# Stores of gathered rows in blocks of 128 nodes, loads in parts of 112 and 13 partitions

## The reference

```python
edge_index = jnp.stack([src, dst])
x = x + gnn0(_layernorm(x), W, bias, src, dst, edge_weight)      # segment_sum(h[dst] * w, src)
x = x + moe0(_layernorm(x), 8 experts 256->256->256, top 2)
x = x + gnn1(_layernorm(x), edge_index, edge_weight, ...)         # 3 layers
x = x + moe1(_layernorm(x), shared 256->1024->256 and 8 experts, top 2)

# gnn1
h = x @ W_in + b_in
for l in range(3):
    msgs = edge_weight[:, None] * h[col]
    pooled = segment_sum(msgs, row) + h
    hid = relu(bn(pooled @ W1[l] + b1[l]))
    h = relu(bn(hid @ W2[l] + b2[l]))
```

## Time and profile before

| | us |
|---|---|
| median of 3 runs | 2988.94 |
| profiled execution | 2990.68 |
| its span | 2988.8 |
| TensorE matmul busy | 2341.4 (78%) |
| VectorE busy | 1330.6 (45%) |
| ScalarE busy | 946.7 (32%) |
| POOL busy | 1418.9 (47%) |
| mean granted clock of TensorE | 0.889 |

### The profile page before, as it was taken

One profiled execution on the slowest core, in us unless ns is written; L12 is line 12 of the kernel. 1 busy time (PEld: TensorE's weight loads), 2 busy tenths in 40 slices (PEclk: granted clock), 3 DMA queues, 4 the chain that ended last, 5 costly groups with the idle time before them and its releaser, 6 DMA issues. The chain is left out here.

```text
span 2988.8 us, 52339 instructions
## 1 busy us (share of the span) xinstructions
PE 2341.4 (78%) x14004; PEld 2098.9 (70%) x14004; DVE 1330.6 (45%) x3733; ACT 946.7 (32%) x2732; POOL 1418.9 (47%) x1465
## 2 busy tenths in 40 slices
PE   1989959999868766776567766567775899999999
PEld 0789959888767635675446766356664689999988
DVE  6789976666443353444334443434443441111122
ACT  4368858788012241000120000300000433333332
POOL 1377767776004355777417777147775001111142
PEclk9999979999859978888789897788986799999999
DMA  2100023333029833333313333133333249999932
GB/s 77 40 4 3 3 65 102 105 105 98 15 82 301 288 105 91 104 104 105 67 64 105 104 105 105 20 110 105 104 105 72 64 163 327 326 328 326 310 91 61
DMA packets 243386, 363.22 MB, mean 122 GB/s; under 512 B 57437, under 2 KB 188486, under 8 KB 242886
## 3 DMA queue, kind: packets, MB, share of 16 engines
q1 hardware_dynamic: 173780, 194.88, 20.1%
q0 software_dynamic: 66240, 163.71, 19.8%
q10 hardware_dynamic: 3250, 3.20, 0.3%
HBM read 322.49 MB, written 38.69 MB: 121 GB/s over the span
## 5 line engine op out<-in xcount | busy, mean ns | idle before, releaser
L749 POOL DMA_INDIRECT z_or_messages<-h_rows,agg_idx x768 | 729.6, 950 | 358.4 <-issue 224.9
L780 PE MATMUL ps<-z_or_messages 128*128 128x125 f32 x3072 | 484.7, 322 | 284.0 <-DMA z_or_messages<-h_rows,agg_idx 238.8
L780 PEld LDWEIGHTS ps<-z_or_messages 128*128 128x128 f32 x3072 | 450.7, 232 | 324.3 <-issue 250.7
L807 DVE TENSOR_TENSOR h_features<-h_features,ps 128x250 f32 x384 | 159.2, 414 | 514.8 <-PE ps L780 477.0
L722 ACT CAST agg_idx<-slots 128x4 int32 x264 | 51.7, 196 | 1042.5 <-PE ps L780 541.2
L1380 POOL DMA_INDIRECT moe_room<-h_rows,moe_inverse x112 | 106.0, 946 | 558.1 <-PE ps L1470 394.0
L749 POOL DMA_INDIRECT agg_room<-h_rows,agg_idx x256 | 248.9, 972 | 96.7 <-issue 70.8
L574 POOL DMA_INDIRECT payloads<-pay_st,idx_st x192 | 215.4, 1122 | 164.5 <-DMA idx_st<-slot_i 112.4
L1638 ACT ACTIVATE moe_room<-ps,moe_b 128x128 f32<-128x128 f32 x560 | 163.2, 367 | 366.4 <-PE ps L1482 366.4
L1482 PE MATMUL ps<-moe_room 128*128 128x128 f32 x2240 | 272.9, 277 | 7.0 <-issue 4.5
L1482 PEld LDWEIGHTS ps<-moe_room 128*128 128x128 f32 x2240 | 260.5, 193 | 13.5 <-issue 8.0
(11 more groups left out here) (285 smaller groups left out, 3263.2 us busy)
## 6 DMA issues: line engine op xcount, KB each, us to landing
moe_room<-in_L_ffn_W1p_dram SPq DMA_DIRECT2D x56, 1024.0 KB, 6.7
moe_room<-in_L_ffn_W2p_dram SPq DMA_DIRECT2D x56, 1024.0 KB, 7.6
moe_room<-in_L_ffn_w_dram SPq DMA_DIRECT2D x112, 256.0 KB, 5.0
expert_out<-moe_room SPq DMA_DIRECT2D x112, 128.0 KB, 6.0
z_or_messages<-h_rows,agg_idx POOLq DMA_INDIRECT x768, 2.7
h_rows<-moe_xn SPq DMA_DIRECT2D x10, 625.0 KB
h_rows<-layer_rows SPq DMA_DIRECT2D x10, 625.0 KB
agg_room<-h_rows,agg_idx POOLq DMA_INDIRECT x256
```

Source lines behind the costliest of these rows:

```text
L749: self.pg.nc.gpsimd.indirect_dma_start(self.G[:, k, :], None, self.pg.H, bass.IndirectOffsetOnAxis(ap=self.idx[:, k:k + 1], axis=0)).then_ ...
L780: last = nc.tensor.matmul(out[:, c, :], self.G[:, k, c * 128:(c + 1) * 128], self.S[:, k, :], start=(u == 0), stop=(u == PAIR - 1))
L807: nc.vector.tensor_tensor(a, a, p, ALU.add).then_inc(self.s_acc, 1)
```

## The change

Two things are changed.

1. The loads of src, dst, edge_weight and x go through `spread`: one transfer for partitions 0 to 111 (EVEN = 125 // 16 * 16 = 112) and one for 112 to 124. The waits are for twice the count.
2. The rows that are gathered in the network (three times: at the end of the first mixture and in layers 0 and 1) are made in 25 blocks of 128 consecutive nodes, the last of 53, and stored with one transfer each. In the mixture a block is made with the chunk that completes it, and the copies go into `got_second` on all 128 partitions. In the layers the buffers become a ring of ROWS = 10 single blocks, [128, 10, 256], each with a semaphore of its own; the copies wait for the store ten blocks back. A block that reaches into a chunk waits for that chunk's relu.

The first graph layer's rows (L322) and the rows that the two mixtures store for themselves (L1311) stay as they were.

```diff
+ROWS = 10
+ROW_BLOCKS = [(s, min(128, N - s)) for s in range(0, N, 128)]
+EVEN = P // 16 * 16
...
+def spread(eng, dst, src, sem):
+    for part in (slice(0, EVEN), slice(EVEN, P)):
+        eng.dma_start(dst[part], src[part]).then_inc(sem, 16)
...
-                sp.dma_start(src_i[:], src.rearrange("(p j) -> p j", p=P)).then_inc(ld_edge, 16)
-                sp.dma_start(dst_i[:], dst.rearrange("(p j) -> p j", p=P)).then_inc(ld_edge, 16)
-                sp.dma_start(slot_f[:], edge_weight.rearrange("(p j) -> p j", p=P)).then_inc(ld_edge, 16)
-                sp.dma_start(pg.X[:], x.rearrange("(j p) d -> p j d", p=P)).then_inc(ld_x, 16)
+                spread(sp, src_i[:], src.rearrange("(p j) -> p j", p=P), ld_edge)
+                spread(sp, dst_i[:], dst.rearrange("(p j) -> p j", p=P), ld_edge)
+                spread(sp, slot_f[:], edge_weight.rearrange("(p j) -> p j", p=P), ld_edge)
+                spread(sp, pg.X[:], x.rearrange("(j p) d -> p j d", p=P), ld_x)
...
-                dve.wait_ge(ld_edge, 48)
+                dve.wait_ge(ld_edge, 96)
...
-                act.wait_ge(ld_x, 16)
+                act.wait_ge(ld_x, 32)
...
+            ends = [0] + [sum(s0 + n <= c0 + m for s0, n in ROW_BLOCKS) for c0, m in CHUNKS]
+            self.row_blocks = [range(a, b) for a, b in zip(ends, ends[1:])]
...
-            for j in range(NT):
+            for j, (s0, n) in enumerate(ROW_BLOCKS):
                 sp.wait_ge(self.s_ro, j + 1)
-                sp.dma_start(pg.H[j * P:(j + 1) * P, :], self.rows[:, j, :]).then_inc(self.s_rst, 16)
-            sp.wait_ge(self.s_rst, 16 * NT)
+                sp.dma_start(pg.H[s0:s0 + n, :], self.got_second[0:n, j, :]).then_inc(self.s_rst, 16)
+            sp.wait_ge(self.s_rst, 16 * len(ROW_BLOCKS))
...
-                    last = nc.tensor.matmul(ps[0:P, 6 + j % 2, 0:D], net.h[:, k, j * P:(j + 1) * P], net.W[:, 1, k, :],
+                    last = nc.tensor.matmul(ps[0:n, 6 + j % 2, 0:D], net.h[:, k, s0:s0 + n], net.W[:, 1, k, :],
...
-                a.copy(self.rows[:, j, :], ps[0:P, 6 + j % 2, 0:D]).then_inc(self.s_ro, 1)
+                a.copy(self.got_second[0:n, j, :], ps[0:n, 6 + j % 2, 0:D]).then_inc(self.s_ro, 1)
...
-        self.rows = sb("rows2", [P, 2, U, D])
+        self.rows = sb("rows2", [128, ROWS, D])
...
-        for j in range(NT):
-            if j * P % CH == 0:
-                pe.wait_ge(ready, KD * (j * P // CH + 1))
+        for j, (s0, n) in enumerate(ROW_BLOCKS):
+            pe.wait_ge(ready, KD * -(-(s0 + n) // CH))
...
-            if j % U == 0 and q >= 2:
-                dve.wait_ge(self.s_st[q % 2], 16 * (q // 2))
+            if j >= ROWS:
+                dve.wait_ge(self.s_st[j % ROWS], 16 * (j // ROWS))
...
-        for q in range(NT // U):
-            sp.wait_ge(self.s_row, U * (q + 1))
-            sp.dma_start(self.pg.H[q * U * P:(q + 1) * U * P, :].rearrange("(j p) d -> p j d", p=P),
-                         self.rows[:, q % 2, :, :]).then_inc(self.s_st[q % 2], 16)
-        for h in range(2):
-            sp.wait_ge(self.s_st[h], 16 * ((NT // U + 1 - h) // 2))
+        for j, (s0, n) in enumerate(ROW_BLOCKS):
+            sp.wait_ge(self.s_row, j + 1)
+            sp.dma_start(self.pg.H[s0:s0 + n, :], self.rows[0:n, j % ROWS, :]).then_inc(self.s_st[j % ROWS], 16)
+        for u in range(ROWS):
+            sp.wait_ge(self.s_st[u], 16 * ((len(ROW_BLOCKS) - u + ROWS - 1) // ROWS))
```

More of the change, by code:

```diff
@@ L1559, in product, with rows @@
                 last.then_inc(self.s_p, 1)
-        def rows(c, j0, n):
+        def rows(c):
             pe.wait_ge(self.s_h, (c + 1) * KD)
-            for j in range(j0, j0 + n):
+            for j in self.row_blocks[c]:
+                s0, n = ROW_BLOCKS[j]
                 if j >= 2:
@@ L1576, in net_tensor @@
             if c:
-                rows(*self.groups[c - 1])
-        rows(*self.groups[G - 1])
+                rows(c - 1)
+        rows(G - 1)
     def net_psum(self, c, fo, n):
@@ L1648, in net_scalar, with rows @@
         a, ps, net = self.pg.nc.scalar, self.pg.ps, self.net
-        def rows(c, j0, n):
-            for j in range(j0, j0 + n):
+        def rows(c):
+            for j in self.row_blocks[c]:
+                n = ROW_BLOCKS[j][1]
                 act.wait_ge(self.s_r, j + 1)
-                a.copy(self.rows[:, j, :], ps[0:P, 6 + j % 2, 0:D]).then_inc(self.s_ro, 1)
+                a.copy(self.got_second[0:n, j, :], ps[0:n, 6 + j % 2, 0:D]).then_inc(self.s_ro, 1)
         act.wait_ge(net.s_w, net.loads)
@@ L1675, in net_scalar @@
             if c:
-                rows(*self.groups[c - 1])
-        rows(*self.groups[-1])
+                rows(c - 1)
+        rows(len(self.groups) - 1)
     def vector(self, dve):
@@ L1867, in __init__ @@
         self.s_out, self.s_tr, self.s_row, self.s_zero = (sem(n) for n in ("relu_out", "trd", "row", "zeroed"))
-        self.s_st = [sem(f"st{s}") for s in range(2)]
+        self.s_st = [sem(f"st{s}") for s in range(ROWS)]
         self.G = KD * len(CHUNKS)
@@ L1956, in rows_product @@
             for k in range(KD):
-                last = self.pg.nc.tensor.matmul(self.pg.ps[0:P, j % BANKS, 0:D], src[:, k, j * P:(j + 1) * P],
+                last = self.pg.nc.tensor.matmul(self.pg.ps[0:n, j % BANKS, 0:D], src[:, k, s0:s0 + n],
                                                 weight[:, k, :], start=(k == 0), stop=(k == KD - 1))
@@ L1967, in rows_out @@
     def rows_out(self, dve):
-        for j in range(NT):
+        for j, (s0, n) in enumerate(ROW_BLOCKS):
             dve.wait_ge(self.s_tr, j + 1)
-            q = j // U
-            if j % U == 0 and q >= 2:
-                dve.wait_ge(self.s_st[q % 2], 16 * (q // 2))
-            self.pg.nc.vector.tensor_copy(self.rows[:, q % 2, j % U, :], self.pg.ps[0:P, j % BANKS, 0:D]
+            if j >= ROWS:
+                dve.wait_ge(self.s_st[j % ROWS], 16 * (j // ROWS))
+            self.pg.nc.vector.tensor_copy(self.rows[0:n, j % ROWS, :], self.pg.ps[0:n, j % BANKS, 0:D]
                                           ).then_inc(self.s_row, 1)
     def rows_store(self, sp):
-        for q in range(NT // U):
-            sp.wait_ge(self.s_row, U * (q + 1))
-            sp.dma_start(self.pg.H[q * U * P:(q + 1) * U * P, :].rearrange("(j p) d -> p j d", p=P),
-                         self.rows[:, q % 2, :, :]).then_inc(self.s_st[q % 2], 16)
-        for h in range(2):
-            sp.wait_ge(self.s_st[h], 16 * ((NT // U + 1 - h) // 2))
+        for j, (s0, n) in enumerate(ROW_BLOCKS):
+            sp.wait_ge(self.s_row, j + 1)
+            sp.dma_start(self.pg.H[s0:s0 + n, :], self.rows[0:n, j % ROWS, :]).then_inc(self.s_st[j % ROWS], 16)
+        for u in range(ROWS):
+            sp.wait_ge(self.s_st[u], 16 * ((len(ROW_BLOCKS) - u + ROWS - 1) // ROWS))
     def rows_add(self, dve, X):
```

## The result

The changed kernel takes 2958.53 us, the median of 4 runs (2956.87 to 2963.87), against 2988.63 before in the same company (2987.89 to 2990.93, 4 runs); ratio 0.9896, 95% interval 0.9884 to 0.9908. The forecast was 2958.6. The profiled execution took 2959.41 us with a span of 2957.6, 31.2 less than before.

A forecast was written before the change was run, and what follows sets the result against it. It took each stage's own last chain before its barrier as the bound, in the first stage x's transfer. Terms -19.7 + 0.4 - 5.5 - 5.5 = -30.3 us, from the median 2988.94, gave 2958.6, range 2949 to 2968.

The forecast's parts named there:

- The bound and the engines: First stage bound by x's transfer; a transfer uses the largest number of engines up to 16 that divides its partitions.
- Rival A: First stage: splitting x brings nothing and only the layers gain, -10.6 us, so 2978 us; chance 6%.
- the direct price: First stage: VectorE's 2.4 us wait for the edges goes, so its first scan ends at 43.0 instead of 45.44.
- x: First stage: x split over 16 engines lands at 19.3 us instead of 39, and VectorE goes on 19.7 us sooner.
- 12.1 us at the expert loop's 315 GB/s: First stage: time for the 3.8 MB of x and edges on 16 engines, at the rate seen in the expert loop.
- 4.7 for the zeroing: First stage: POOL's zeroing of a table takes 4.7 us of every engine while x loads.
- the bound of 15.0: First stage: the gain if the table's zeroing slows x by twice the 4.7 us.
- The mixture's end: End of the first mixture: last store of 53 rows on one engine takes 2.3 us, tail 2.9 + 2.3 against 4.8, +0.4.
- The layers: Layers 0 and 1: no row store queues and copies keep TensorE's pace, -5.5 us in each.
- the 2.9 of fixed time: Tail from last copy to next load: what remains of 4.8 us without the stores' 1.1 and 0.8.
- the 0.4 for the semaphores: Layers' tail: 0.4 us for eight more semaphores that SP waits on.
- The clock rivals B and C: Second mixture: B, clock rises sooner, 2945 us, chance 5%; C, it rises later, 2999 with 80 us, chance 3%.

The follow-up runs named there:

- the run with 64 + 61: The changed kernel with x loaded in 64 + 61 partitions instead of 112 + 13; 3015.82 us (one run).
- the split tail: The changed kernel with the last block's 53 rows stored as 48 + 5 rows in two transfers; 2953.53 us, ratio 0.9876.

## Why the prediction was right, and where its terms were not

**The bound and the engines: right.** That 125 partitions use five engines and 112 use sixteen was read from shares of 0.34 and 0.94; the run with 64 + 61 and the packet counts show it. Rival A is out: loads alone gave 14.6 us. The rule of the Trainium skill on transfers to disjoint partition halves (DMA: Bandwidth & Descriptors, "Rules for kernel authors"), that they are not worth the trouble, fails here, because its premise that each already uses all the engines does not hold for 125 partitions.

**Edges: the direct price was right** in the changed kernel's trace (scan's end 42.92 against 43.0; in the other runs with split edges up to 43.95), but their larger part was missed. Split edges also let x be complete 4.7 us sooner, by the reading above because unsplit ones load five of the engines more than the rest.

**x: mis-sized by 4.1 us, the largest error.** The failed step is "12.1 us at the expert loop's 315 GB/s", plus 4.7 for the zeroing. Without the zeroing 3.8 MB take 21.69 - 2.5 = 19.2 us, and the zeroing costs 1.7 us. The two errors had opposite signs, +7.1 and -3.0. Of the 7.1 some 3.7 are the rate (240 GB/s would make it 15.8 us) and the remaining 3.4 the slow end behind 17 us, which the forecast did not have at all. The gain was 15.6 us, near the bound of 15.0, but that bound had been drawn for a dearer zeroing, which did not come.

**The mixture's end:** +0.4 was forecast, -0.3 measured at the tail. What the row block costs that moves to the last group can't be read: the stretch around it varies by 6 us.

**The layers: right in kind, 0.6 us short each.** From the first copy to the next load 6.1 and 6.0 us were won, forecast 5.5. The tail after the last copy was put at 5.6 and is 4.65; 2.3 for the 53 rows is what the split tail gave back, so the over-estimate lies in the 2.9 of fixed time and the 0.4 for the semaphores. No row stood behind that 0.4; the layers' tails are 0.14 us longer than the mixture's, where one semaphore is waited on (0.2 with 48 + 5). The third and fourth stretch gained 0.9 to 1.0 us more, ahead of the copies; that is not explained, and among kernels that are alike there this part varies by 1.1 and 0.6 us. Likewise the 0.9 us at the end of the span.

**The sum** was met within 1 us because x came 4.1 us (at the stage's end 4.5) short and all else gained 5.4 us more than forecast, 1.5 of it in the stretch that varies. The method was right, the exactness was luck. The clock rivals B and C did not come. In the second mixture (columns as in rows 2):

```profile
2360.00:2370.00 10.00, 10.00 (x36) 8.65 (x36) 7.59 (x19) 5.89 (x10) 0.00 (x0) 0.66 0.34 121
```

A mean of 0.66 puts the rise to 1.00 at 2366.8 us, against 2397.2 before by the same working: 30.4 us sooner, and the load that opens the last aggregation came 30.3 us sooner. The last stretch kept its length to 0.9 us.

## What to carry to other kernels

Look at the DMA share while one transfer runs: here 0.34 at full demand meant that the shape of the transfer, not the memory, was the limit, and a split at 112 partitions, a multiple of 16, mended it. Mind the remainder too: 53 leftover rows on one engine cost 2.3 us at each barrier more than 48 + 5. Do not take the full rate from another part of the kernel as the rate of the mended transfer, allow for an end at which some engines are done before others, and let the consumer wait in pieces where it works in pieces.

## What the runs showed of the hardware that was not expected

Sixteen engines reading x in rows of 1 KB move 230 to 262 GB/s, twice and not three times what five of them do, while their busy share is 1.1; with rows that lie together, 25 KB to a partition, it is 230 GB/s from 7 to 11 us at a share of 0.89 to 0.93. In the same kernel other loads run at 315 over 400 us, and with the zeroing beside x the same engines move 386 GB/s in all from 13 to 15 us. None of three things explains it by itself, neither the place of the rows, nor the zeroing, nor the weights behind x. The end of x in one piece is slow besides: the engines do not finish together (with the weights away, a share of 0.56 from 19 to 21 us and of 0.08 behind it), while x in five groups, with 367 GB/s in all from 17 to 19 us, shows no such end. A transfer on few engines also delays a wide one that follows: x lands 4.7 us later behind 0.6 MB of unsplit edges (one run).
